# A gated attention and mixture-of-experts block on one core: plain adds for the shared blocks, loops written out, and a new order of the first loads and conversions

## What is computed

```python
x = x + tanh(g_xattn) * xattn(layernorm(x), ctx)     # x: 4 x 512 x 512, ctx: 4 x 512 x 256
x = x + tanh(g_ffn) * ffn(layernorm(x))

def xattn(t, f):                                     # Wq, Wk: 128 x 256
    q, k = f @ Wq.T + bq, f @ Wk.T + bk
    att = softmax(q @ k.T)                           # 512 x 512 per batch
    return t @ att.T

def ffn(x):                                          # D = 512, H = 352, 8 experts, 2 per token
    shared = (silu(x @ Wg_s) * (x @ Wu_s)) @ Wd_s
    p = sigmoid(x @ Wr + br + rb)
    v, i = top_k(p, 2); v = v / sum(v)
    return shared + sum over the two chosen experts e of v_e * (silu(x @ Wg[e]) * (x @ Wu[e])) @ Wd[e]
```

## Time and profile before

| what | value |
|---|---|
| median of three runs | 511.6 us (512.7, 510.02, 511.6) |
| span of the profiled execution, first to last instruction | 510.6 us |
| TensorE busy | 460.4 us (90%) |
| DVE, ACT, POOL busy | 237.0, 222.8, 191.9 us |
| mean granted TensorE clock | 0.973 |
| attention | to about 132 us of the span |
| shared blocks | to about 243 us |
| routed blocks | to about 499 us |

### The profile page before, as it was taken

One profiled execution on the slowest core, in us unless ns is written; L12 is line 12 of the kernel. 1 busy time (PEld: TensorE's weight loads), 2 busy tenths in 40 slices (PEclk: granted clock), 3 DMA queues, 4 the chain that ended last, 5 costly groups with the idle time before them and its releaser, 6 DMA issues.

```text
span 510.6 us, 9678 instructions
## 1 busy us (share of the span) xinstructions
PE 460.4 (90%) x2861; PEld 282.3 (55%) x2862; DVE 237.0 (46%) x421; ACT 222.8 (44%) x369; POOL 191.9 (38%) x254
## 2 busy tenths in 40 slices
PE   5659999999899599886999999999999999999980
PEld 3325556565556266543566666666666666666650
DVE  3575959586789984454122222222222222222220
ACT  2755868686565255543233333333333333333320
POOL 1560111111132832224444444444444444544431
PEclk9998999999999799999799999999999999999997
DMA  5945322222768377775444444444444444444433
GB/s 178 339 153 186 122 85 82 82 91 78 233 188 212 106 198 181 200 191 106 92 80 88 84 83 83 82 82 82 82 82 82 82 82 82 82 82 82 83 41 42
DMA packets 38422, 59.65 MB, mean 117 GB/s; under 512 B 4736, under 2 KB 22592, under 8 KB 38400
## 3 DMA queue, kind: packets, MB, share of 16 engines
q0 software_dynamic: 11040, 24.65, 27.8%
q1 hardware_dynamic: 27360, 34.70, 20.8%
HBM read 36.27 MB, written 23.07 MB: 116 GB/s over the span
## 4 chain that ended last, share of the span: by engine, by line
PE 54%; DMA 19%; issue 7%; DVE 6%; ACT 5%; POOL 3%; SPq 2%; POOLq 1%; DVEq 0%; ACTq 0%
DMA out_rows<-y,idx_s 16%; PE bank L1111 9%; PE bank L1114 9%; PE bank L1112 9%; PE bank L970 7%; PE bank L1122 5%; PE bank L1123 5%; PE bank L1124 5%; DVE W L746 2%; POOL W L474 1%; DVE negmax L721 1%; DMA stage<-in_L_ffn_Wd_s 1%; DMA xg<-x2n_rows,idx_g 1%; DMA x2n_rows<-W 1%; ACT W L518 1%
## 5 line engine op out<-in xcount | busy, mean ns | idle before, releaser
L447 POOL DMA_INDIRECT out_rows<-y,idx_s x55 | 91.8, 1669 | 170.1 <-ACT y L602 119.2
L1111 PE MATMUL bank<-W,xT 128*128 x312 | 95.3, 313 | 1.1 <-issue 1.0
L1112 PE MATMUL bank<-W,xT 128*128 x312 | 95.3, 313 | 0.0
L602 ACT ACTIVATE y<-bank,wcol 128x512 f32<-128x512 f32 x55 | 37.8, 687 | 101.0 <-DMA out_rows<-y,idx_s 58.5
L922 DVE TENSOR_TENSOR h<-bank,silu_g 128x352 f32<-128x352 f32 x55 | 28.7, 523 | 104.4 <-ACT silu_g L607 104.4
L607 ACT ACTIVATE silu_g<-bank 128x352 f32<-128x352 f32 x55 | 25.5, 464 | 116.8 <-PE bank L1114 116.7
L926 DVE TENSOR_TENSOR hT<-bank,hT 128x384 f16<-128x384 f32 x55 | 30.6, 557 | 90.2 <-ACT hT L611 90.0
L1114 PE MATMUL bank<-W,xT 128*128 x312 | 72.0, 313 | 0.0
L1122 PE MATMUL bank<-W,hT 128*128 (+1 forms) x165 | 64.1, 389 | 7.7 <-DVE hT L926 7.7
L1123 PE MATMUL bank<-W,hT 128*128 (+1 forms) x165 | 63.9, 387 | 0.0
L1124 PE MATMUL bank<-W,hT 128*128 (+1 forms) x165 | 63.5, 385 | 0.0
(11 more groups left out here) (142 smaller groups left out, 764.9 us busy)
## 6 DMA issues: line engine op xcount, KB each, us to landing
stage<-in_L_ffn_Wg SPq DMA_DIRECT2D x16, 352.0 KB, 3.1
stage<-in_L_ffn_Wu SPq DMA_DIRECT2D x16, 352.0 KB, 4.0
W<-in_x SPq DMA_DIRECT2D x4, 1024.0 KB, 7.4
stage<-in_L_ffn_Wd SPq DMA_DIRECT2D x16, 256.0 KB, 4.5
out_rows<-W SPq DMA_DIRECT2D x16, 256.0 KB, 2.1
x2n_rows<-W SPq DMA_DIRECT2D x16, 256.0 KB, 2.0
W<-in_ctx SPq DMA_DIRECT2D x4, 512.0 KB, 5.2
stage<-in_L_ffn_Wd SPq DMA_DIRECT2D x16, 96.0 KB, 5.4
```

What stands on the lines that cost most here:

```text
L447: g.indirect_dma_start(out, bass.IndirectOffsetOnAxis(ap=idx_s[:, i:i + 1], axis=0), y[:, i, :], None, compute_op=ALU.add).then_inc(s_sc, 16)
L602: a.activation(y[:, i, :], PY[:, :], ACT.Copy, scale=wcol[:, bass.ds(n, 1)]).then_inc(s_y, 1)
L1111: t.matmul(bank[:, 0:H], hi, gu_w(off, HI, m, c), start=(c == 0), stop=False)
L1112: t.matmul(bank[:, 0:H], hi, gu_w(off, LO, m, c), start=False, stop=False)
```

## The change

1. **First loads.** x of batch 0 is loaded in four quarters with a semaphore each, and `x_stats(0, q)` waits for its own quarter. The two biases are loaded from ACT's queue under a semaphore of their own, and the projections wait for them alone. `load_x(1)` and `load_ctx(1)` come before the shared weights on SP, the pad store of zeros before `load_x(2)`. The first routed halves are loaded after the stores of batch 1 in place of before those of batch 0.
2. **Shared conversions.** ACT's high half becomes four pieces, one ahead of each quarter of `step(0, 1, 2)`. The low halves on DVE become eight pieces, four in step 0 and four in step 1. POOL's high half moves behind `scale_x(1)`.
3. **Shared adds.** `add_shared` issues a plain accumulating DMA from POOL, with no row numbers and no wait for the add before. The scatters and gathers of the routed blocks read their row numbers straight from `tgt` and `tok`. `s_sc` becomes two semaphores.
4. **Loops written out** on all five queues, the 39 routed blocks among them.
5. **Logits** stay in PSUM for all batches; `logits_out` goes. `block_experts` runs before `block_onehots`. Two waits of ACT and DVE for stores at the end of a step go.

```diff
+            for q in range(NQ):
+                sp.dma_start(x_sb[:, q * D:(q + 1) * D], x_v[0, :, q, :]).then_inc(s_x0[q], 16)
+            for dst, src in ((gates[:, 0:1], g_x.partition_broadcast(P)), (gates[:, 1:2], g_f.partition_broadcast(P)),
...
+            load_x(1)
+            load_ctx(1)
             sp.wait_ge(s_zero, 3)
             for k in (1, 0):
...
-                if k == 1:
-                    load_x(1)
-            load_ctx(1)
+            sp.dma_start(out[T:T + P, :], y[:, 0, :]).then_inc(s_pad, 16)
             load_x(2)
+            load_ctx(2)
             load_x(3)
...
+            store(0)
+            load_ctx(3)
+            store(1)
             for k in range(2):
                 stage_routed(0, k)
-            store(0)
-            load_ctx(3)
-            with sp.Fori(1, B - 1) as b:
-                store(b)
+            store(2)
...
+            def gather(n):
+                i = n % 2
                 need(pool, s_xt, n - NT - 1)
-                g.tensor_copy(idx_g[:, i:i + 1], tok[:, bass.ds(n - NT, 1)]).then_inc(s_idxg, 1)
-                wait_apart(pool, s_idxg, n - NT + 1)
                 g.indirect_dma_start(xg[:, i, :], None, x2n_rows,
-                                     bass.IndirectOffsetOnAxis(ap=idx_g[:, i:i + 1], axis=0)).then_inc(s_xg[i], 16)
+                                     bass.IndirectOffsetOnAxis(ap=tok[:, n - NT:n - NT + 1], axis=0)).then_inc(s_xg[i], 16)
+
+            def add_shared(n):
+                pool.wait_ge(s_y, n + 1)
+                g.dma_start(out[n * P:(n + 1) * P, :], y[:, n % 2, :], accum_op=ALU.add).then_inc(s_sc[n % 2], 16)
+
+            def scatter(n):
+                if n == NT:
+                    all_landed(pool, s_sc, NT)
+                else:
+                    pool.wait_ge(s_sc[(n - 1) % 2], 16 * ((n - 1) // 2 + 1))
+                pool.wait_ge(s_y, n + 1)
+                g.indirect_dma_start(out, bass.IndirectOffsetOnAxis(ap=tgt[:, n - NT:n - NT + 1], axis=0), y[:, n % 2, :],
+                                     None, compute_op=ALU.add).then_inc(s_sc[n % 2], 16)
...
+            step(None, 1)
             pool.wait_ge(s_stg[0], 64)
             g.tensor_scalar(W[:, SHARED_AT:SHARED_AT + HALF], stage[:, 0, :], WSCALE, None, ALU.mult).then_inc(s_shh[0], 1)
-            step(None, 1)
...
+            for n in range(POS_BLOCK + 1):
+                add_shared(n)
 
             pool.wait_ge(s_b1h, 1)
             for f, z in enumerate((tok_id[:, :], whi, wlo)):
...
+            def shared_piece(q):
+
+                if q == 0:
+                    act.wait_ge(s_stg[1], 64)
+                o, n = SHARED_AT + 2 * HALF + q * (HALF // NQ), HALF // NQ
+                a.activation(W[:, o:o + n], stage[:, 1, q * n:(q + 1) * n], ACT.Copy, scale=WSCALE).then_inc(s_shh[1], 1)
+
             def step(s2, s1, nx):
                 for q in range(NQ):
+                    if s2 == 0:
+                        shared_piece(q)
...
-            act.wait_ge(s_par, 16 * PARS)
+            act.wait_ge(s_bqk, 16 * 2)
             project(0, 0)
             project(0, 1)
+            act.wait_ge(s_par, 16 * PARS)
             a.activation(tanh_g[:, :], gates[:, :], ACT.Tanh).then_inc(s_tanh, 1)
             a.activation(wr16[:, HI], wr_sb[:, :, :], ACT.Copy, scale=WSCALE).then_inc(s_wrh, 1)
-            act.wait_ge(s_stg[1], 64)
-            o = SHARED_AT + 2 * HALF
-            a.activation(W[:, o:o + HALF], stage[:, 1, :], ACT.Copy, scale=WSCALE).then_inc(s_shh[1], 1)
...
                     if nx is not None:
                         x_stats(nx, q)
+                    if s2 in (0, 1):
+                        shared_piece(1 - s2, q)
                     if s1 is not None and q > 0:
                         probs_lo(s1, q - 1)
...
                 elif n == 5:
+                    block_experts()
                     block_onehots()
-                    block_experts()
...
-            for k in (1, 0):
-                convert(SHARED_AT, k, s_shh[k], 0)
-            with dve.Fori(0, B - 2) as b:
+            for b in range(B - 2):
                 step(b, b + 1, b + 2)
...
-            PER_TURN = 12
-            turns = (NB - NT) // PER_TURN
-            with pe.Fori(0, turns) as r:
-                before = expert(PER_TURN * r + (NT - 1))
-                for k in range(PER_TURN):
-                    off = expert(PER_TURN * r + (NT + k))
-                    blk(PER_TURN * r + (NT + k), k % 2, PER_TURN // 2 * r + ((k + 1) // 2 + 1), off, before)
-                    before = off
-            before = expert(NT + PER_TURN * turns - 1)
-            for n in range(NT + PER_TURN * turns, NB):
+            pe.wait_ge(s_cvl, 2 * E)
+
+            before = SHARED_AT
+            for n in range(NT, NB):
                 off = expert(n)
```

More of the change, by code:

```diff
@@ L266, in two_before, with all_landed @@
         def two_before(eng, s, b, q):
-            if q > 1:
-                eng.wait_ge(s, NQ * b + q - 1)
+            need(eng, s, NQ * b + q - 1)
         def stored_before(eng, s, b, q):
-            if q > 1 or isinstance(b, int) and b > 0:
-                eng.wait_ge(s[q % 2], 16 * (NQ // 2 * b + q // 2))
+            n = NQ * b + q
+            if n > 1:
+                eng.wait_ge(s[n % 2], 16 * (n // 2))
+        def all_landed(eng, s, n):
+            for i in range(2):
+                eng.wait_ge(s[i], 16 * ((n + 1 - i) // 2))
         def all_stored(eng, s, b):
@@ L382, in _ @@
             stage_routed(1, 1)
-            with sp.Fori(2, E) as e:
+            for e in range(2, E):
                 for k in range(2):
@@ L463, in _ @@
             all_stored(pool, s_st_x2, B - 1)
-            pool.wait_ge(s_pad, 16)
             LEAD = 4
-            for n in range(2):
-                scatter(n, n % 2)
-            with pool.Fori(1, POS_BLOCK // 2) as r:
-                for i in range(2):
-                    scatter(2 * r + i, i)
+            for n in range(POS_BLOCK + 1):
+                add_shared(n)
             pool.wait_ge(s_b1h, 1)
@@ L475, in _ @@
                                 ALU.mult).then_inc(s_bf, 1)
-            with pool.Fori(POS_BLOCK // 2, (NT - LEAD) // 2) as r:
-                for i in range(2):
-                    scatter(2 * r + i, i)
+            for n in range(POS_BLOCK + 1, NT - LEAD):
+                add_shared(n)
+            pool.wait_ge(s_pad, 16)
             all_stored(pool, s_st_n, B - 1)
             pool.wait_ge(s_route, 1)
-            for n in range(NT - LEAD, NT - LEAD + 2):
-                scatter(n, n % 2)
-                gather(n + LEAD, n % 2)
-            with pool.Fori((NT - LEAD) // 2 + 1, (NB - LEAD - 1) // 2) as r:
-                for i in range(2):
-                    scatter(2 * r + i, i)
-                    gather(2 * r + i + LEAD, i)
-            for n in range(NB - LEAD - 1, NB):
-                scatter(n, n % 2)
+            for n in range(NT - LEAD, NB):
+                if n < NT:
+                    add_shared(n)
+                else:
+                    scatter(n)
                 if n + LEAD < NB:
-                    gather(n + LEAD, n % 2)
+                    gather(n + LEAD)
         @block.scalar
@@ L585, in step @@
                     silu(0 if s1 is not None else 1)
-                if s2 is not None and nx is not None:
-                    all_stored(act, s_st_n, s2)
             def convert(slot, k, loads):
@@ L658, in _ @@
             act.wait_ge(s_route, 1)
-            with act.Fori(PEELED // 2, NT // 2 - 1) as r:
-                for k in range(2):
-                    blk(2 * r + 1 + k, 1 - k)
-                    convert(r + 1, k, r + 3)
+            for n in range(PEELED, NT - 1):
+                blk(n, n % 2)
+                routed_half(n + 1)
             blk(NT - 1, 1, turn=True)
-            with act.Fori(NT // 2, (NB - 1) // 2) as r:
-                for i in range(2):
-                    blk(2 * r + i, i, turn=True)
+            for n in range(NT, NB - 1):
+                blk(n, n % 2, turn=True)
             blk(NB - 1, 0)
@@ L952, in _ @@
                 routed_half(n + 1)
-            with dve.Fori(PEELED // 2, NT // 2 - 1) as r:
-                for k in range(2):
-                    blk(2 * r + 1 + k)
-                    convert((r + 1) * SLOT, k, s_cvh, 2 * r + 2 + k)
+            for n in range(PEELED, NT - 1):
+                blk(n)
+                routed_half(n + 1)
             blk(NT - 1, turn=True)
-            with dve.Fori(NT // 2, (NB - 1) // 2) as r:
-                for i in range(2):
-                    blk(2 * r + i, turn=True)
+            for n in range(NT, NB - 1):
+                blk(n, turn=True)
             blk(NB - 1)
@@ L1161, in _ @@
             pe.wait_ge(s_wrl, 1)
-            with pe.Fori(0, B - 2) as b:
+            for b in range(B - 2):
                 step(b, b + 1, b + 2)
-            pe.wait_ge(s_cvl, 2)
+            pe.wait_ge(s_shl, 2 * NQ)
             step(B - 2, B - 1, None)
```

97 lines of the change are left out of this document (42 added, 55 removed).

## The result

The changed kernel takes 489.46 us (median of four runs, 488.11 to 491.81) against 512.15 (510.02 to 513.72): ratio 0.956, 95% interval 0.9523 to 0.9597, 22.7 us less. Measured again later beside three of the experiments it took 488.39 against 512.23 (six runs, 0.9583, 0.9523 to 0.9644), 23.8 us less. The ratios count only executions within 1.5% of the fastest of their kernel and are not the quotients of the two medians. The forecast was 485.7, the range 481 to 496.

The account below looks back on a forecast made before the run. TensorE, busy nine tenths of the span, was taken to bound the kernel, so only its idle or slow places could be regained: 6.5 + 9.8 + 8.0 + 1.6 = 25.9 us off 511.6 gives 485.7 us, range 481 to 496.

Parts of the forecast that it names:

- Start: From the start to silu of block 2: 6.5 us earlier, including 2.7 from ACT's first copy of x starting sooner.
- The hole: TensorE's 4.43 us idle before batch 1's energies: 3.6 us come back, plus 2.4 from the slow clock after it.
- The pieces: Shared-weight conversions cut into pieces on ACT and DVE in steps 0 and 1: 3.0 us lost.
- The 0.8 for the loops: Loops written out gain about 0.4 us at each of two step borders.
- Multiplies: POOL's three multiplies in the shared blocks still delay DVE's conversion of half 6: 2.3 us lost.
- It slips in after one multiply: DVE's conversion of half 6 (L810) waits for one of POOL's three multiplies: 2.3 us; chance 0.33.
- the first rival: DVE's conversion of half 6 (L810) waits for all three of POOL's multiplies: 492.4 us; chance 0.28.
- The other blocks: Silu 2 to 15 without harm from the multiplies: 80.3 us in place of 92.45, 12.1 us gained.
- Hidden: Plain shared adds land within two blocks, 11.9 us, and cost nothing, because their bytes are the same.
- Border: Silu 15 to silu 16: gather 16 issued three blocks ahead cuts 14.25 us to 6.3, gaining 8.0.
- Routed blocks: TensorE's pauses and slower first issues at loop turns and exit go: 1.6 us gained.
- the other side: Rival: written-out code is fetched anew, 0.7 us for each of 39 routed blocks, 513 us, no gain; chance 0.03.

Follow-up runs that it names:

- experiment 3: The changed kernel with the two bias loads issued by SP again, ahead of the quarters of x: 488.21 us (ratio 0.9559).
- experiment 10: On top of experiment 9, seven matmuls on a matrix of ones run on TensorE while it waits for ctx: 482.72 us (ratio 0.946).
- Experiment 5: The changed kernel with the shared weights converted as before the change, without pieces on ACT or DVE: 500.99 us (ratio 0.9798).
- experiment 2: The changed kernel with POOL's three multiplies given to DVE, in blocks 6 and 7: 486.45 us (ratio 0.9511).
- experiment 9: The changed kernel with the multiplies on DVE in block 8, tables one block later, bias loads on SP: 482.94 us (ratio 0.9459).
- experiment 6: The changed kernel with shared adds as indirect DMAs, each waiting until the one before landed: median 497.47 us (490.2 to 500.6).
- experiment 7: The same kernel as experiment 6, indirect shared adds in series, run once more: 497.82 us.
- experiment 1: The changed kernel with block_onehots ahead of block_experts again in block 5, as before the change: 488.77 us (ratio 0.9585).
- experiment 4: The changed kernel with each plain shared add waiting until the add before it has landed: 487.86 us (ratio 0.9547).

## Why the prediction was right in sum, and where its sizes were off

**Start (6.5; 7.4 measured).** ACT's first copy moved 1.2 us (from 19.02 to 17.78) and not 2.7. ctx lands 1.1 later behind the biases on ACT's queue (experiment 3), which the prediction did not count: it moved two issues off SP and asked nothing of where they went. The first projection also took 6.45 in place of 5.74, a length that changes from execution to execution (experiment 10). The hole and the slow clock behind it came back about as taken: 4.43 to 1.19, and full clock. Experiment 5 ties them to the conversions. The pieces cost about half of the 3.0 taken. The 0.8 for the loops had no row behind it and no run tests it; with the pieces at 1.5, about 2 us are left for the loops and whatever else changed. That the sum came within a microsecond is luck: its errors of size cancel.

**Multiplies (2.3; 4.4 to 6.0 measured, silu 6 to 10 against the prediction's own 26.15 without them).** This term was mis-sized most. "It slips in after one multiply" was right for L810 in the changed kernel, and I stopped there. There are three multiplies, so DVE gives way three times, and the operations behind L810 (lane one-hots, the next conversion) read SBUF twice as well. The sum of DVE's losses is 5.0 us, TensorE's waits and the clock come on top. Experiments 2 and 9 take the contention away, and 4.2 us (30.6 to 26.4) come back in the second although DVE now does the multiplies itself. The full wait that was the first rival did not occur for L810 in the changed kernel, but the time lies midway between it (492.4) and the forecast. It did occur in experiments 6 and 7 (8.18 and 8.58 us), where the multiplies come a block later. Both outcomes occur in this kernel, by where the chain of multiplies falls, and the nearly equal chances of the two (0.33 and 0.28) were fair.

The Trainium skill (SBUF — State Buffer, Who interferes with whom) has the two-input operations right: the one that comes second stands fully still, and this case's rows show it, a multiply going from 2.3 to 4.4 us. It lists tensor_scalar among the operations that can take both ports, which agrees with the eoff row, held for 6.33 and 7.35 us. Who comes next when both engines have work queued, the section does not say, and the kind of DVE's operation does not settle it: a conversion with two inputs takes 4.17 us in one trace and 8.18 in another. In the seven traces where the engines take turns, POOL had stood idle 0.6 to 0.9 us for DVE just before the first multiply; in the four where an operation of DVE is held through the chain (experiments 1, 6 and 7), POOL came to it straight from issuing a DMA. No run isolates this, and the cause stays open.

**The other blocks (80.3 for silu 2 to 15 without the multiplies; 81.3 in experiment 9, its multiplies on DVE included).** The base was right. In the first profile about 1.1 us more lie between silu 10 and 15 than in the best (31.1 against 30.0), with ACT's two waits of 0.6 and 0.8 for stage; what delays these loads in some executions stays open.

**Adds.** "Hidden" was right and the reason half right. A series of plain adds costs nothing, a series of indirect ones does (experiments 4, 6, 7): late adds in some executions, and the later multiplies in both traces. The loops and copies of row numbers of the kernel before were not put back on POOL, so their share is open.

**Border (8.0; 6.7 measured).** Gather 16 is early. The form of the adds is 3.1 us of it in experiment 7 and nothing in 6; which edit brought the rest no run shows. Block 16 takes 6.6 to 7.9 us instead of the 6.3 taken: a first routed block is not a steady one.

**Routed blocks (1.6; 1.9 in the trace, 2.5 for TensorE's loop alone).** Right. Of the other side, code written out at 0.7 us a block, nothing is seen: blocks of 6.29 us.

The sum was 25.9, the medians give 22.7 and 23.8, the traces 20.5, with the longest of the four executions. Against the sum these traces lack 3.7 us at the multiplies, 1.3 between silu 10 and 15, 1.3 at the border and 0.3 ahead of silu 6; the start and the routed blocks gave 1.2 more.

## What to carry to other kernels

When an operation slips between the pieces of another engine's chain, count the pieces, not the slip: each piece can displace whatever stands next, and the same operation can be held through the whole chain when the chain comes at another moment (experiments 6 and 7). A stall that is moved off one instruction lands on the next ones in its queue; here undoing the swap cost nothing that the times show, while taking the rival engine's work away brought about 2 us (experiment 2), and 5 with the later place and the biases (experiment 9). And small loads that leave one queue still arrive ahead of something on another: look what lands later.

## What the runs showed of the hardware

- DVE operations with two inputs in SBUF and POOL's multiplies with two inputs alternate one by one in seven traces: 4.17, 3.92 and 4.02 us in place of 2.42, 2.27 and 2.42, multiplies of 4.4 in place of 2.3. In two others such an operation waits through all three multiplies, 8.18 and 8.58 us, and a 1x39 tensor_scalar does in two more, 6.33 and 7.35 us, where it takes 0.17 alone. What decides between the two is not shown.
- A plain accumulating DMA of 256 KB takes 0.86 to 1.16 us to issue and 3.9 to 6.6 to land, median 5.3; the indirect one, in a series, 1.54 to 3.64 and 4.5 to 9.7, median 5.8 (experiment 7).
- Two bias loads of 0.5 KB each on ACT's queue make ctx, issued at the same time on SP's, 0.8 to 1.1 us late (5.2 to 5.5 in place of 4.4).
- The first eight matmuls of 512 columns take 5.6 to 6.6 us in eleven profiles and 3.70 in three, one of them with seven matmuls ahead, at a granted clock of 1.00 in the rows that were read (8.96 to 15.40 in the first profile, 8.70 to 12.40 in experiment 1). The granted clock alone does not show this loss.
